# The filter network of a fused long convolution: weights and biases of two layers scaled ahead, biases added by a matmul, rounding out of PSUM

## The reference

```
h = sin(freq * (z @ w1 + b1))
h = sin(freq * (h @ w2 + b2))
h = sin(freq * (h @ w3 + b3))
h = (h @ wo) * decay
```

## Time and profile before

| | us |
|---|---|
| median of 3 runs | 938.78 (938.49 to 938.9) |
| the profiled execution | 938.39 |
| its span, first to last instruction | 936.6 |
| PE busy in it | 924.2 (99%) |
| DVE, POOL, ACT busy | 742.2, 694.4, 682.8 |

### The profile page before, as it was taken

The page is one execution under the profiler, slowest core; times in us unless marked ns, Lnnn a source line. Parts: engine busy times, 40 slices in busy tenths (PEclk is TensorE's granted clock), DMA queues, the critical chain, the costliest instruction groups (busy, mean ns, idle before and its releaser), DMA issues.

```text
span 936.6 us, 18917 instructions
## 1 busy us (share of the span) xinstructions
PE 924.2 (99%) x5318; PEld 811.9 (87%) x5318; DVE 742.2 (79%) x2195; ACT 682.8 (73%) x1154; POOL 694.4 (74%) x599
## 2 busy tenths in 40 slices
PE   8999999999999999999999999999999999999996
PEld 6888888888888888888888888888888888888885
DVE  5778778787888788788787787878887887887887
ACT  4547786787777777777777867877777777777786
POOL 3786787777877777877877877777777778778775
PEclk9999999999999999999999999999999999999998
DMA  7967999999999998999999999999999999999965
GB/s 245 349 170 224 246 262 262 286 261 271 272 260 236 286 291 266 254 283 245 279 282 217 286 299 250 263 288 250 280 272 244 272 258 278 289 244 263 266 178 202
DMA packets 91311, 244.10 MB, mean 261 GB/s; under 512 B 17056, under 2 KB 41504, under 8 KB 83104
## 3 DMA queue, kind: packets, MB, share of 16 engines
q1 hardware_dynamic: 73440, 235.34, 84.8%
q10 hardware_dynamic: 17856, 8.59, 8.8%
HBM read 176.53 MB, written 67.37 MB: 260 GB/s over the span
## 4 chain that ended last, share of the span: by engine, by line
PE 98%; DVE 1%; issue 0%; ACT 0%; POOL 0%; DVEq 0%; POOLq 0%
PE ps_c L783 37%; PE ps_u L783 33%; PE ps_z L783 28%; DVE z_sb L1001 0%; DVE z_sb L1164 0%; DVE z_sb L965 0%; DVE ul L1088 0%; ACT uh L595 0%; ACT z_sb L587 0%; DVE z_sb L978 0%; DVE z_sb L993 0%; DVE z_sb L973 0%; POOL rstd L445 0%; DVEq L157 0%; DVE toep L1004 0%
## 5 line engine op out<-in xcount | busy, mean ns | idle before, releaser
L496 POOL TENSOR_TENSOR zl<-z_sb,zh 128x1024 fp32r<-128x1024 f32 x127 | 305.4, 2404 | 135.8 <-ACT zh L638 135.8
L783 PE MATMUL ps_z<-uh,toep 128*128 128x512 f32 x768 | 257.7, 390 | 0.1
L684 ACT ACTIVATE out_sb<-z_sb,shift,gain 128x256 f32<-128x256 f32 x488 | 253.1, 591 | 4.4
L783 PE MATMUL ps_u<-toep,xh 128*128 128x256 f32 x1024 | 241.9, 317 | 1.3 <-DVE toep L1004 1.3
L595 ACT ACTIVATE uh<-ps_u 128x1024 fp32r<-128x1024 f32 x128 | 130.2, 1017 | 152.0 <-PE ps_z L783 150.8
L1061 DVE CUSTOM_DVE_ANT_0 products<-z_sb,ps_c 128x256 bf16<-128x256 f32 x504 | 181.5, 416 | 65.8 <-PE ps_c L783 65.5
L783 PE MATMUL ps_c<-zh,wh 128*128 128x512 f32 x504 | 202.8, 402 | 0.0
L1051 DVE SCALAR_TENSOR_TENSOR z_sb<-x_sb,par,ps_z 128x1024 f32<-128x1024 f32 x128 | 163.7, 1279 | 46.7 <-ACT out_sb L684 40.9
L1088 DVE TENSOR_TENSOR ul<-ps_u,uh 128x1024 fp32r<-128x1024 f32 x128 | 152.9, 1195 | 57.9 <-ACT uh L595 57.8
L783 PE MATMUL ps_c<-zh,wl 128*128 128x512 f32 x504 | 197.2, 391 | 0.0
L783 PE MATMUL ps_u<-toep_whole,xt_sb 128*128 128x128 f32 x1024 | 196.5, 273 | 0.0
(11 more groups left out here) (104 smaller groups left out, 928.9 us busy)
## 6 DMA issues: line engine op xcount, KB each, us to landing
xt_sb<-xt_in SPq DMA_DIRECT2D x64, 1024.0 KB, 10.5
x_sb<-x_in SPq DMA_DIRECT2D x128, 512.0 KB, 7.6
out<-out_sb SPq DMA_DIRECT2D x122, 512.0 KB, 6.2
w_sb<-wt_in SPq DMA_DIRECT2D x64, 256.0 KB, 5.6
toep_whole<-filters_padded SPq DMA_DIRECT2D x63, 256.0 KB, 7.2
everyone<-partition_moments ACTq DMA_DIRECT2D x61, 128.0 KB, 5.2
out<-z_sb SPq DMA_DIRECT2D x6, 256.0 KB, 2.7
out<-z_sb SPq DMA_DIRECT2D x2, 512.0 KB, 3.5
```

Source lines behind the costliest of these rows:

```text
L496: nc.gpsimd.tensor_tensor(low, z_sb[:, r, h], high.bitcast(F32), ALU.subtract)\
L684: last = nc.scalar.activation(to[:, k, b], z_sb[:, r, h, k, b], ACT.Identity, bias=shift[:, r, g:g + 1], scale=gain[:, r])
L783: return nc.tensor.matmul(o, a, b, start=start, stop=stop)
```

## The change

The angles of the second and third layer come out of PE complete, in turns. With f = freq/2pi, a column of w2 and w3 (one unit) and its bias are multiplied by that unit's f ahead; PSUM then holds h @ (w f) + b f, and rounding and difference read PSUM.

Three rows are added to the unused partitions of `par` where the first layer's weights lie: b2 and b3 as rows (partitions 64 and 65), freq as a row (partition 96), and two columns that select one of the two bias rows. PE spreads the frequency row over all partitions by a matmul with one row of the constant 1/128 into `ps_z`; ACT copies it out, times 128/2pi, to `freq_row`; POOL multiplies the bias rows and w2 by it; DVE multiplies w3 by it, behind its work for the first layer. PE adds the bias by a matmul with two rows (`bias_rows` against a broadcast selecting column, start of the accumulation), one for each half, ahead of the layer's matmuls. The layers alternate between two banks of PSUM (`layer_bank`). The first layer computes its angle as before. `scaled`, `freq_row` and `bias_rows` are pieces of `z_sb` as well.

```diff
-COL_W2, COL_W3, COL_WO = (COL_FREQ + 1 + i * P for i in range(3))
+COL_SELECT = COL_FREQ + 1
+COL_W2, COL_W3, COL_WO = (COL_SELECT + 2 + i * P for i in range(3))
+BIAS_ROWS, FREQ_ROW = slice(64, 66), slice(96, 97)
...
+        freq_row = early[0][:, 0:P]
+        scaled = early[0][:, P:3 * P].rearrange("p (l n) -> p l n", l=2)
+        bias_rows = early[0][BIAS_ROWS, 3 * P:4 * P]
...
+        def layer_bank(layer, i):
+            return ps_u[:, layer % 2, i, 0, 0:P]
... POOL, behind its memsets
+            pool.wait_ge(slide_clear, 1)
+            pool.wait_ge(first_landed, 16)
+            pool.wait_ge(freq_row_ready, 1)
+            nc.gpsimd.tensor_tensor(bias_rows, par[BIAS_ROWS, COL_W1:COL_W1 + P], freq_row[BIAS_ROWS, :], ALU.mult)\
+                .then_inc(bias_scaled, 1)
+            pool.wait_ge(weights_landed, 16)
+            pool.wait_ge(bias_scaled, 1)
+            nc.gpsimd.tensor_tensor(scaled[:, 0], par[:, COL_W2:COL_W2 + P], freq_row, ALU.mult)\
+                .then_inc(second_scaled, 1)
... ACT
+            act.wait_ge(freq_spread, 1)
+            nc.scalar.activation(freq_row, ps_z[:, 0, 0, 0:P], ACT.Copy, scale=P / (2.0 * math.pi))\
+                .then_inc(freq_row_ready, 1)
+            act.wait_ge(layer_done, 2)
+            act.wait_ge(bias_turns_ready, 1)
+            nc.scalar.activation(arg[:, HALVES[1]], layer_bank(0, 1), ACT.Identity,
+                                 bias=bias_turns[:, 0:1], scale=freq_turns[:, 0:1]).then_inc(second_arg, 1)
             for layer in range(3):
-                act.wait_ge(layer_done, 2 * layer + 2)
-                if layer == 0:
-                    act.wait_ge(bias_turns_ready, 1)
-                nc.scalar.activation(arg[:, HALVES[1]], ps_u[:, 0, 1, 0, 0:P], ACT.Identity,
-                                     bias=bias_turns[:, layer:layer + 1], scale=freq_turns[:, 0:1])\
-                    .then_inc(second_arg, 1)
                 for i, half in enumerate(HALVES):
-                    act.wait_ge(reduced, 5 * layer + 4 + 2 * i)
+                    act.wait_ge(reduced, 4 * layer + 4 + 2 * i)
... PE
+            mm(ps_z[:, 0, 0, 0:P], ones[FREQ_ROW, :].bitcast(F32), par[FREQ_ROW, COL_W1:COL_W1 + P], True, True)\
+                .then_inc(freq_spread, 1)
             pe.wait_ge(weights_landed, 16)
             for layer, col in enumerate((COL_W2, COL_W3, COL_WO)):
                 keep_warm(WARM_LAYER)
+                if layer < 2:
+                    pe.wait_ge(bias_scaled, 1)
+                    select = par[BIAS_ROWS, COL_SELECT + layer:COL_SELECT + layer + 1].broadcast_to([2, P])
+                    for i in range(2):
+                        mm(layer_bank(layer + 1, i), bias_rows, select, True, False)
+                    pe.wait_ge((second_scaled, third_scaled)[layer], 1)
                 for i, half in enumerate(HALVES):
                     pe.wait_ge(hid_ready, 2 * layer + 1 + i)
-                    mm(ps_u[:, 0, i, 0, 0:P], par[:, col:col + P], hid[:, half], True, True)\
-                        .then_inc(layer_done, 1)
+                    weights = scaled[:, layer] if layer < 2 else par[:, col:col + P]
+                    mm(layer_bank(layer + 1, i), weights, hid[:, half], layer == 2, True).then_inc(layer_done, 1)
... DVE
+            dve.wait_ge(layer_done, 1)
+            nc.vector.tensor_scalar(arg[:, HALVES[0]], layer_bank(0, 0), par[:, COL_BIAS:COL_BIAS + 1],
+                                    freq_turns[:, 0:1], ALU.add, ALU.mult).then_inc(reduced, 1)
             for layer in range(3):
-                dve.wait_ge(layer_done, 2 * layer + 1)
-                nc.vector.tensor_scalar(arg[:, HALVES[0]], ps_u[:, 0, 0, 0, 0:P],
-                                        par[:, COL_BIAS + layer:COL_BIAS + layer + 1],
-                                        freq_turns[:, 0:1], ALU.add, ALU.mult).then_inc(reduced, 1)
                 for i, half in enumerate(HALVES):
-                    if i == 0:
-                        dve.wait_ge(reduced, 5 * layer + 2)
+                    if layer > 0:
+                        dve.wait_ge(layer_done, 2 * layer + 1 + i)
+                    elif i == 0:
+                        dve.wait_ge(reduced, 2)
                     else:
-                        dve.wait_ge(second_arg, layer + 1)
-                    nc.vector.tensor_scalar(turns[:, half], arg[:, half], ROUND_MAGIC, ROUND_MAGIC,
+                        dve.wait_ge(second_arg, 1)
+                    angle = layer_bank(layer, i) if layer > 0 else arg[:, half]
+                    nc.vector.tensor_scalar(turns[:, half], angle, ROUND_MAGIC, ROUND_MAGIC,
                                             ALU.add, ALU.subtract).then_inc(reduced, 1)
...
-                    nc.vector.tensor_tensor(part[:, half], arg[:, half], turns[:, half], ALU.subtract)\
+                    nc.vector.tensor_tensor(part[:, half], angle, turns[:, half], ALU.subtract)\
                         .then_inc(reduced, 1)
+                if layer == 0:
+                    dve.wait_ge(weights_landed, 16)
+                    dve.wait_ge(freq_row_ready, 1)
+                    nc.vector.tensor_tensor(scaled[:, 1], par[:, COL_W3:COL_W3 + P], freq_row, ALU.mult)\
+                        .then_inc(third_scaled, 1)
```

More of the change, by code:

```diff
@@ L238, in build @@
         second_arg = sem("second_arg")
+        freq_spread = sem("freq_spread")
+        freq_row_ready = sem("freq_row_ready")
+        second_scaled = sem("second_scaled")
+        bias_scaled = sem("bias_scaled")
+        third_scaled = sem("third_scaled")
         hid_ready = sem("hid_ready")
@@ L795, in _ @@
             for i, half in enumerate(HALVES):
-                mm(ps_u[:, 0, i, 0, 0:P], par[:, COL_W1:COL_W1 + P],
+                mm(layer_bank(0, i), par[:, COL_W1:COL_W1 + P],
                    par[:, COL_ZT + half.start:COL_ZT + half.stop], True, True).then_inc(layer_done, 1)
+            mm(ps_z[:, 0, 0, 0:P], ones[FREQ_ROW, :].bitcast(F32), par[FREQ_ROW, COL_W1:COL_W1 + P], True, True)\
+                .then_inc(freq_spread, 1)
             pe.wait_ge(weights_landed, 16)
@@ L961, in _ @@
                                     None, ALU.mult).then_inc(bias_turns_ready, 1)
+            dve.wait_ge(layer_done, 1)
+            nc.vector.tensor_scalar(arg[:, HALVES[0]], layer_bank(0, 0), par[:, COL_BIAS:COL_BIAS + 1],
+                                    freq_turns[:, 0:1], ALU.add, ALU.mult).then_inc(reduced, 1)
             for layer in range(3):
-                dve.wait_ge(layer_done, 2 * layer + 1)
-                nc.vector.tensor_scalar(arg[:, HALVES[0]], ps_u[:, 0, 0, 0, 0:P],
-                                        par[:, COL_BIAS + layer:COL_BIAS + layer + 1],
-                                        freq_turns[:, 0:1], ALU.add, ALU.mult).then_inc(reduced, 1)
                 for i, half in enumerate(HALVES):
-                    if i == 0:
-                        dve.wait_ge(reduced, 5 * layer + 2)
-                    else:
-                        dve.wait_ge(second_arg, layer + 1)
-                    nc.vector.tensor_scalar(turns[:, half], arg[:, half], ROUND_MAGIC, ROUND_MAGIC,
+                    if layer > 0:
+                        dve.wait_ge(layer_done, 2 * layer + 1 + i)
+                    elif i == 0:
+                        dve.wait_ge(reduced, 2)
+                    else:
+                        dve.wait_ge(second_arg, 1)
+                    angle = layer_bank(layer, i) if layer > 0 else arg[:, half]
+                    nc.vector.tensor_scalar(turns[:, half], angle, ROUND_MAGIC, ROUND_MAGIC,
                                             ALU.add, ALU.subtract).then_inc(reduced, 1)
-                    dve.wait_ge(reduced, 5 * layer + 3 + 2 * i)
+                    dve.wait_ge(reduced, 4 * layer + 3 + 2 * i)
                     if layer > 0:
                         dve.wait_ge(hid_ready, 2 * layer - 1 + i)
-                    nc.vector.tensor_tensor(part[:, half], arg[:, half], turns[:, half], ALU.subtract)\
+                    nc.vector.tensor_tensor(part[:, half], angle, turns[:, half], ALU.subtract)\
                         .then_inc(reduced, 1)
+                if layer == 0:
[3 more added lines that the diff above has]
+                        .then_inc(third_scaled, 1)
             dve.wait_ge(rest_landed, 16)
@@ L984, in _ @@
                 dve.wait_ge(layer_done, 7 + i)
-                nc.vector.tensor_tensor(filt[:, P + P * i:P + P * (i + 1)], ps_u[:, 0, i, 0, 0:P],
+                nc.vector.tensor_tensor(filt[:, P + P * i:P + P * (i + 1)], layer_bank(3, i),
                                         par[:, COL_DECAY + P * i:COL_DECAY + P * (i + 1)], ALU.mult)\
@@ L1262 @@
         params[ORDER:P, COL_BIAS + i] = a["L0_conv_Y" + name].reshape(-1)
+    for row, name in ((BIAS_ROWS.start, "b2"), (BIAS_ROWS.start + 1, "b3"), (FREQ_ROW.start, "freq")):
+        params[row, COL_W1:COL_W1 + ORDER] = a["L0_conv_X" + name].reshape(-1)
```

(3 more changed lines are left out.)

## The result

The changed kernel takes 942.72 us (median of 9 runs, 939.16 to 942.97), the kernel before 938.78 (9 runs, 938.49 to 938.99): ratio 1.0037, 95% interval 1.0028 to 1.0046, so 3.9 us slower by the medians. The profiled execution has 942.72 us and a span of 940.9. Eight of the nine runs lie between 942.1 and 943.0, one at 939.16.

A forecast was written before the change was run, and what follows sets the result against it. PE was taken to bound the kernel, with the filter network's layer chain ahead of it. Terms +0.79 and -0.76 gave +0.03 us: 938.42 from the profiled 938.39, 938.8 against the median 938.78; range 938.0 to 939.8.

The forecast's parts named there:

- +0.79: Ahead of the second layer: scaling the weights via PE, ACT and POOL delays its first matmul from 5.41 to 6.20 us.
- runs four passes of 0.11 (two bias matmuls): PE ahead of the second layer: bias passes run from 5.69 to about 6.13 us, before POOL's weights arrive.
- just hidden by 0.06: Ahead of the third layer: PE's queue is through at 7.68, before the first matmul at 7.74 us.
- the clock comes late: Rival, second layer: PE's clock rises only behind the bias passes, +0.6 in all, 939.4 us; chance 0.08.
- PE does more work, not less: Argument against the late-clock rival, for the stretch between 4.05 and 5.41 us where the clock rises.
- +0.03: At the output matrix's first matmul: the whole sum, +0.79 - 0.76 us, passed on to the end.
- gain of 0.38 a layer: Second and third layer: 0.44 saved by dropping DVE's angle, less 0.06 for rounding out of PSUM; together -0.76 us.
- -0.88: Second and third layer: the favourable end of the -0.76 us gained by no longer forming the angle.
- -0.06 a layer: Second and third layer: favourable end for the difference reading PSUM, itself forecast as no change.
- POOL and DVE take turns: Rival, 5.18 to 6.7 us: DVE's SBUF instructions and POOL's products exclude each other, +0.42, 939.2; chance 0.27 with dearer POOL.
- carry everything behind it one to one: From the output matrix's first matmul on: any shift moves the first image product and the end by the same amount.

The follow-up runs named there:

- full_bias: The changed kernel with only the bias matmuls on 128 rows, the spread still on one row: 940.44 us.
- full_both: The changed kernel with the spreading and bias matmuls on all 128 rows, same passes and waits: 938.95 us.
- freq_columns: The changed kernel with frequencies loaded on 128 rows by their own DMA, DVE scaling bias rows, full-row bias matmuls replacing layer warming: 938.82 us.

## Why the prediction was wrong

Forecast 938.8, range 938.0 to 939.8; measured 942.72.

The step that failed is PE's part in the term "+0.79" in front of the second layer: "runs four passes of 0.11 (two bias matmuls)". The spread was priced at the early pace (0.43), but the bias passes at the pace that the earlier trace rows show only from 6.12 on, and the two warming matmuls ahead of them at nothing, as PE was to wait for POOL until 5.69. In the changed kernel spread and warming filled PE's queue, and with the gap behind them the bias passes started at 6.21, though POOL's bias product was done at 6.07. These four took 1.15 us to the next start, not 0.44, and all passes up to 15.1 us stayed at half pace. The second layer's matmul came at 7.36 (6.20 forecast, 5.41 before): +1.95 instead of +0.79. The same queue then set the third layer's matmul, 10.51 (7.74 forecast), where the forecast had it just hidden by 0.06, and the output's, 12.38 (9.28 forecast). The output's own passes and copies added 1.1 more before 18.95.

The warning was in the earlier trace rows, which show the clock still low in that stretch, and I had a rival for it, "the clock comes late", with a chance of 0.08. But I dismissed it with "PE does more work, not less": by the busy column that is true (10.00 of 10 us), and it is the wrong measure. I also priced it for one layer (+0.6), not for the whole network, and nothing in the sum allowed for a gap where the number of rows changes.

The rest of the sum held in its single durations, but not in its hand-overs. The trace of `full_bias` shows it. There the profiled execution had the clock up early (pair of 0.73 at 4.85), with the spread still on one row:

```profile
4.85 0.73 PE L808 MATMUL ps_c<-ones 128*128 128x512 f32 x2
5.93 0.71 PE L808 MATMUL ps_u<-par,z_sb 128*128 128x128 f32 x4 [0.34 <-POOL z_sb L449]
6.61 0.71 PE L808 MATMUL ps_u<-z_sb 128*128 128x128 f32 x4
...
8.24 0.92 PE L808 MATMUL ps_u<-z_sb 128*128 128x128 f32 x4
...
9.75 0.49 PE L808 MATMUL ps_u<-z_sb,par 128*128 128x128 f32 x2
```

The weight load of the matmuls at 6.61 (PEld), and POOL's two products ahead of it:

```profile
6.61 0.52 PEld L808 LDWEIGHTS ps_u<-z_sb 128*128 128x128 f32 x4 [0.16 <-POOL z_sb L453]
...
5.42 0.46 POOL L449 TENSOR_TENSOR z_sb<-par,z_sb 128x128 f32<-128x128 f32 x1 [4.13 <-ACT z_sb L603]
6.02 0.54 POOL L453 TENSOR_TENSOR z_sb<-par,z_sb 128x128 f32<-128x128 f32 x1
```

Here the weights of the second layer's matmul did wait for POOL's second product, as forecast, but until 6.61 and not 6.20. POOL starts 0.18 us behind ACT's copy and 0.14 behind its own first product (in the changed kernel too: 5.44 to 5.62, 6.07 to 6.21), where the forecast had 0.04 for both; the copy started 0.09 late and the second product took 0.54 instead of 0.47. The term is +1.20. The steps behind it are 1.63 and 1.51 (1.54 forecast), so the output matrix comes 0.50 later than before and not 0.03, and the time is 0.50 longer too (938.89 against 938.39). So even with the clock up early the change would have cost about half a microsecond. The medians of `full_both` and of the kernel before, 938.95 and 938.78, lie too near each other to tell +0.03 from that. In its own trace the output matrix comes at 10.12, 0.87 later than before, in an execution 0.87 longer.

The gain of 0.38 a layer is there where PE isn't in the way: the output matrix 1.51 behind the third layer in `full_both` (8.61 to 10.12), 1.52 in `freq_columns`, instead of 1.92. In the changed kernel it is worth nothing, since the chain no longer passes through DVE. A slip without effect: the lower end of the gain, -0.88, leaves out the -0.06 a layer that the text grants the difference; with it the end is -1.00.

Of the rivals, "POOL and DVE take turns" had the direction right (DVE's instructions between SBUF tiles get longer beside POOL's products) and no effect on the result: in the changed kernel it adds 0.11 and 0.21 to two DVE instructions off the path. The first image product did carry everything behind it one to one: +4.26 there and +4.3 in the span.

Left open: why one run in nine of the changed kernel (939.16), one in six with only the spread on full rows (939.0) and one in six with more warming (939.64) are as fast as with the clock up early, and why, the other way round, two in ten of `full_both` (940.18, 940.29) and one of 17 of the kernel before in a later series (940.55) are slow. If these times tell the clock, thin passes make the late rise likely, not certain, and full ones don't exclude it. No trace shows one of the short runs of the changed kernel; that of `full_bias` is of its short kind (938.89, first image product at 15.20), so it is no evidence for its median of 940.44.

## What to carry to other kernels

Before PE's clock is up, price each matmul at half pace and look at how many rows its operands have: matmuls with one or two rows in that stretch can keep all others at 1.2 GHz, and spreading the same product over 128 rows with zeros costs no pass and took 3.8 us away here, in gaps and in clock. Judge the clock by the durations of equal matmuls early and late, and the waits by the distance between starts, not by PE's busy share or the granted clock. Give a hand-over to POOL its own price, from a row of POOL. And a chain shortened on DVE is worth nothing if the edit feeds PE's queue so that PE becomes the chain.

## What the hardware showed that was not expected

- TensorE stayed at 1.2 GHz for 10 us that the trace shows as busy without a break, with thin passes between full ones (the thin ones took 2.3 of the 10 us; pairs of 512-wide matmuls 1.20 instead of 0.71 us).
- Changing between a thin and a full operand leaves PE without work for about 0.28 us. The weights of the one-row passes load 0.22 us after those of the former passes (on 128 rows they load without a gap, and the same pass started at 4.17 instead of 4.33). It is the same behind the two-row passes:

```profile
4.33 0.50 PEld L808 LDWEIGHTS ps_z<-par,ones 1*128 1x128 f32 x2 [0.22 <-issue]
...
7.35 0.93 PEld L808 LDWEIGHTS ps_u<-z_sb 128*128 128x128 f32 x4 [0.22 <-issue]
```

- POOL starts later behind its releaser than the other engines on this path: 0.18 us behind ACT's copy and 0.14 behind its own product, where DVE, ACT and PE took 0.02 to 0.04.
- A DMA that reads one DRAM row for 128 partitions (64 KB) took 4.9 us to land and held up the 195.5 KB load of the first parameters on the other queue by 2.1 us; as 128 rows lying apart, the same 64 KB landed in 2.8 us and delayed it by 0.2 to 0.4 us (first passes at 3.38 and 3.56 instead of 3.18).
